# A graph attention layer: two edges to a byte before the transposes, the E row kept in PSUM, row sums divided on GpSimd and ScalarE

## The reference

```python
h = jnp.maximum(_layernorm(x, axis=-1), 0.0)
Wh = h @ W
f1 = Wh @ a[:128, 0];  f2 = Wh @ a[128:, 0]
e = jax.nn.leaky_relu(f1[:, None] + f2[None, :], negative_slope=0.2)
e = jnp.where(adj == 0, -jnp.inf, e)
out = x + jax.nn.softmax(e, axis=1) @ Wh
```

## Time and profile before

| | |
|---|---|
| median of three runs | 870.19 us |
| the profiled execution's own time | 872.21 us |
| its span | 870.5 us |
| PE busy | 841.6 us (97%) |
| PEld busy | 773.6 us (89%) |
| DVE busy | 766.2 us (88%) |
| ACT busy | 104.8 us (12%) |
| POOL busy (all of it but 0.9 us is DMA issue) | 137.0 us (16%) |
| queue of the mask loads | 67.13 MB written, 81.3% of 16 engines |
| granted TensorE clock | 0.997 of full |

### The profile page before, as it was taken

The page is one execution under the profiler, slowest core; times in us unless marked ns, Lnnn a source line. Parts: engine busy times, 40 slices in busy tenths (PEclk is TensorE's granted clock), DMA queues, the critical chain, the costliest instruction groups (busy, mean ns, idle before and its releaser), DMA issues.

```text
span 870.5 us, 23030 instructions
## 1 busy us (share of the span) xinstructions
PE 841.6 (97%) x9481; PEld 773.6 (89%) x9481; DVE 766.2 (88%) x1326; ACT 104.8 (12%) x286; POOL 137.0 (16%) x262
## 2 busy tenths in 40 slices
PE   3899999999999999999999999999999999999995
PEld 3788999999999999999999999999999999999995
DVE  4899898998989898898989889898989889898985
ACT  4788700000000000000000000000000000000000
POOL 3111111111111111111111111101110111111000
PEclk9999999999999999999999999999999999999998
DMA  9995699988998889888988998898889889988300
GB/s 219 113 107 52 59 112 87 94 92 80 95 91 90 83 91 95 81 92 87 97 83 90 91 85 92 81 103 83 90 83 94 92 81 94 93 90 82 48 2 15
DMA packets 43275, 75.95 MB, mean 87 GB/s; under 512 B 4720, under 2 KB 6896, under 8 KB 43248
## 3 DMA queue, kind: packets, MB, share of 16 engines
q0 software_dynamic: 38400, 67.13, 81.3%
q1 hardware_dynamic: 4432, 8.39, 2.9%
q10 hardware_dynamic: 416, 0.07, 0.0%
HBM read 272.70 MB, written 4.19 MB: 318 GB/s over the span
## 4 chain that ended last, share of the span: by engine, by line
PE 91%; DVE 6%; ACT 1%; DMA 1%; issue 1%; ACTq 0%; DVEq 0%
PE acc L275 50%; PE acc L279 26%; PE stage L264 13%; DVE wt_ring L620 3%; PE stage L237 1%; DVE stats L556 1%; DMA a_sb<-in_L_gnn_a_dram 1%; PE stage L224 1%; DVE pairs L611 1%; PE stage L252 1%; DVE xn L593 0%; ACT xn L399 0%; ACT wh L414 0%; DVE packed L603 0%; DVE xm L726 0%
## 5 line engine op out<-in xcount | busy, mean ns | idle before, releaser
L620 DVE SCALAR_TENSOR_TENSOR wt_ring<-row,packed,stage 128x512 f32<-128x512 uint8 (+1 forms) x1024 | 695.3, 742 | 74.9 <-PE acc L279 69.1
L275 PE MATMUL acc<-pairs,wt_ring 128*128 128x258 f16 x4096 | 720.2, 274 | 0.4 <-DVE wt_ring L620 0.2
L279 PE MATMUL acc<-pairs,wt_ring 128*128 128x129 f16 x4096 | 698.4, 219 | 0.0
L275 PEld LDWEIGHTS acc<-pairs,wt_ring 128*128 128x128 f16 x4096 | 396.2, 97 | 55.4 <-DVE wt_ring L620 0.4
L279 PEld LDWEIGHTS acc<-pairs,wt_ring 128*128 128x128 f16 x4096 | 399.5, 98 | 4.9
L178 POOL DMA_DIRECT2D masks<-in_adj_dram x252 | 133.2, 529 | 664.7 <-PE stage L264 635.7
L264 PE MATMUL stage<-ident,masks 128*128 128x128 f32 x1024 | 155.3, 275 | 2.0 <-ACT fin L483 2.0
L264 PEld LDWEIGHTS stage<-ident,masks 128*128 128x128 f32 x1024 | 108.7, 141 | 6.0 <-ACT fin L483 2.3
L513 ACT ACTIVATE fin<-acc 128x258 f32<-128x258 f32 x64 | 24.7, 386 | 730.2 <-PE acc L275 730.2
L237 PE MATMUL stage<-wx,ht 128*128 128x130 f32 x128 | 23.5, 311 | 0.7 <-ACT ht L408 0.7
L434 ACT ACTIVATE tmp<-wh,tmp 128x128 f32<-128x128 f32 x64 | 20.4, 390 | 0.4
(11 more groups left out here) (51 smaller groups left out, 80.1 us busy)
## 6 DMA issues: line engine op xcount, KB each, us to landing
masks<-in_adj_dram POOLq DMA_DIRECT2D x256, 256.0 KB, 8.8
out_dram<-xm SPq DMA_DIRECT2D x16, 256.0 KB, 2.1
xm<-in_x_dram SPq DMA_DIRECT2D x3, 1024.0 KB, 15.7
xm<-in_x_dram SPq DMA_DIRECT2D x1, 768.0 KB, 6.5
xm<-in_x_dram SPq DMA_DIRECT2D x1, 256.0 KB, 3.0
wx<-in_L_gnn_W_dram ACTq DMA_DIRECT2D x1, 64.0 KB, 3.2
a_sb<-in_L_gnn_a_dram ACTq DMA_DIRECT2D x1, 1.0 KB, 6.5
```

Of the source, the lines that this page charges most:

```text
L275: return nc.tensor.matmul(acc[:, r, 0:2 * E1], wtv[:, w, r, 1, :], pairv[:, t, :, 0:E1], start=st, stop=end)
L279: return nc.tensor.matmul(acc[:, r, 0:E1], wtv[:, w, r, 0, :], pairv[:, t, 0, 0:E1], start=False, stop=False)
L620: nc.vector.scalar_tensor_tensor(out=wt_ring[:, t % NW, :], in0=e_row, scalar=packed[:, t, 1:2], in1=marks[:, k, :], op0=ALU.max, op1=ALU. ...
```

## The change

**Edges.** The two last rows of each four-row pack (the "second" rows) are multiplied by 200, in place and as 16-bit numbers, and GpSimd adds them as 32-bit integers to the two first ones: a byte then holds a + 200 b. In group 0 and for the first four units of group 1 GpSimd does the multiplication (`second` in its block, L227), from then on ScalarE does, eight units ahead (`second`, L560). The sum is `mix` (L215). TensorE now transposes two 128x128 blocks for a unit (L368), not four. ScalarE reads the 1024 bytes of each partition from PSUM, multiplies by 1.28, adds 0.1 and writes 16-bit numbers to `marks` in SBUF (`unpack`, L549): its low byte is a, its high byte b. VectorE reads the edges from `marks`, with a step of two bytes (L774).

**E row.** `row` and its copy by ScalarE are gone. `spread` (L359) is done once in each group, after its third unit, for the next group; VectorE reads the E row straight from bank 1 or 3 of `stage`. VectorE copies the four values that it needs to `e_next` first (L791). Edges use banks 0 and 2 in the groups from 1 on and bank 0 in group 0, and transposes run two units ahead.

**Rows of output.** `finish` is gone but for the last group. GpSimd adds the halves (`sums`, L262 and L265), VectorE takes the reciprocal after the seventh unit (L848), ScalarE scales the rows after the ninth (`divided`, L583), GpSimd adds x (`outputs`, L272). **Group 0.** GpSimd takes `scaled` (L255) from ScalarE, for groups 1 to 15, and from group 4 on VectorE's half of the normalisation (L236). **Loads.** The second rows of a chunk are loaded when the chunk has been mixed, the first rows when it has been transposed.

The diff, cut to what bears on this:

```diff
--- before.py
+++ after.py
+SECOND = 200.0
+SPLIT = 256.0 / SECOND
+ABOVE = 0.1
...
-        row = sb("row", [P, N], F32)
+        marks = sb("marks", [P, MR, CHUNK], U8)
+        e_next = sb("e_next", [P, PACK], F32)
...
+            def mix(u):
+                c, k = u // KC % NC, u % KC
+                if k == 0 and u >= KC:
+                    pool.wait_ge(adj_loaded[c], (u // UN + (1 if c else 0)) * 2 * 16)
+                if u < UN + KC:
+                    pool.wait_ge(s["second_pool"], u + 1)
+                else:
+                    pool.wait_ge(s["second_ready"], u + 1 - UN - KC)
+                sl = slice(k * P, (k + 1) * P)
+                nc.gpsimd.tensor_tensor(edges4[:, c, 0, :, sl], edges4[:, c, 0, :, sl], edges4[:, c, 1, :, sl],
+                                        ALU.add).then_inc(s["mixed"], 1)
+            def second(u):
...
+                nc.gpsimd.tensor_scalar(twos[:, c, 1, :, sl], twos[:, c, 1, :, sl], SECOND, None, ALU.mult
+                                        ).then_inc(s["second_pool"], 1)
+            def sums(q):
+                pool.wait_ge(s["acc_free"], (q + 1) * PACK)
+                nc.gpsimd.tensor_scalar(fin[:, :, E1:2 * E1], fin[:, :, E1:2 * E1], 1.0 / LOW, None, ALU.mult
+                                        ).then_inc(s["lows_scaled"], 1)
+                pool.wait_ge(s["lows_scaled"], q + 1)
+                nc.gpsimd.tensor_tensor(fin[:, :, 0:E1], fin[:, :, 0:E1], fin[:, :, E1:2 * E1], ALU.add
+                                        ).then_inc(s["sums_ready"], 1)
+            for n in range(NC - 1, NQ * NC - 2):
+                if NC <= n < NQ * NC - NC:
+                    load_first(n + NC)
+                for k in range(KC):
+                    mix((n + 2) * KC + k)
+                if n + 2 + NC < NQ * NC:
+                    load_second(n + 2 + NC)
+                if n >= NC and n % NC == 0:
+                    sums(n // NC - 1)
+                if n >= NC and n % NC == 2:
+                    outputs(n // NC - 1)
...
+            def group(q, bank):
+                for b in range(UN):
+                    pe.wait_ge(s["marked"], q * UN + b + 1)
+                    transposes(b % 2 * 2, (b + 2) % UN, q * UN + b + 2)
+                    unit(q * UN + b, b, q)
+                    if b == 2:
+                        pe.wait_ge(s["weighted"], q * UN * PACK)
+                        pe.wait_ge(s["e_ready"], q + 2)
+                        spread(bank)
...
+            def unpack(bank, u, b):
+                act.wait_ge(s["transposed"], u + 1)
+                if bank or b >= MR:
+                    act.wait_ge(s["weighted"], (u + 1 - MR) * PACK)
+                nc.scalar.activation(split[:, b % MR, :].rearrange("p (s w) -> p s w", s=PACK),
+                                     stage[:, bank, 0:BANK // 2].bitcast(U8).rearrange("p (w s) -> p s w", s=PACK),
+                                     ACT.Copy, scale=SPLIT, bias=ABOVE).then_inc(s["marked"], 1)
+            def second(q, b):
...
+                nc.scalar.activation(twos[:, c, 1, :, sl], twos[:, c, 1, :, sl], ACT.Copy, scale=SECOND
+                                     ).then_inc(s["second_ready"], 1)
...
-            def weights(bank, b, e_row):
-                marks = stage[:, bank, :].bitcast(U8).rearrange("p (w s) -> p s w", s=PACK)
+            def weights(bank, b):
+                edges = marks[:, b % MR, :].rearrange("p (s w h) -> p s h w", s=PACK, h=2)
+                e_row = stage[:, bank, :].rearrange("p (h k) -> p h k", h=2)
...
-            def finish(q, step):
...
+            def rows(q, bank, more=True):
+                dve.wait_ge(s["rowp_ready"], q + 1)
+                if more:
+                    next_group(q + 1)
                 for b in range(UN):
                     u = q * UN + b
-                    dve.wait_ge(s["transposed"], u + 1)
+                    dve.wait_ge(s["marked"], u + 1)
                     dve.wait_ge(s["used"], u - 1)
-                    weights(b % 4, b, e_row)
-                    if 2 <= b <= 4:
-                        finish(q - 1, b - 2)
+                    weights(bank, b)
+                    if b == 6:
+                        dve.wait_ge(s["sums_ready"], q)
+                        nc.vector.reciprocal(inv[:], fin[:, :, Fo]).then_inc(s["inv_ready"], 1)
```

More of the change, by code:

```diff
@@ new lines, in normalise @@
+            def normalise(g):
+                pool.wait_ge(s["ln_ready"], batch_of(g) + 1)
+                pool.wait_ge(s["xt_ready"], g - 1)
+                for r in range(HALF, PACK):
+                    t = g * PACK + r
+                    ins = nc.gpsimd.tensor_scalar(xn[:, g % 2, r * P:(r + 1) * P], xm[:, g, r * P:(r + 1) * P],
+                                                  small[:, 5, t:t + 1], small[:, 6, t:t + 1], ALU.mult, ALU.add)
+                ins.then_inc(s["xn_pool"], 1)
@@ new lines, in load_second, with load_first, scaled @@
+            def load_second(n):
+                pool.wait_ge(s["mixed"], (n - NC + 1) * KC)
+                for r in (2, 3):
+                    load(n // NC, n % NC, r)
+            def load_first(n):
+                pool.wait_ge(s["transposed"], (n - NC + 1) * KC)
+                for r in (0, 1):
+                    load(n // NC, n % NC, r)
+            def scaled(g):
+                pool.wait_ge(s["exps_ready"], g + 1)
+                nc.gpsimd.tensor_tensor(tmp[:, g % 2, :, 0:Fo], wh[:, g * PACK:(g + 1) * PACK, 0:Fo],
+                                        tmp[:, g % 2, :, Fo:E1].to_broadcast([P, PACK, Fo]), ALU.mult
+                                        ).then_inc(s["scaled_ready"], 1)
@@ L189, in _, with outputs, load_rows @@
+            def outputs(q):
+                pool.wait_ge(s["fin_scaled"], q + 1)
+                y = xm[:, q, :].rearrange("p (r k) -> p r k", r=PACK)
+                nc.gpsimd.tensor_tensor(y, fin[:, :, 0:Fo], y, ALU.add).then_inc(s["rows_done"], PACK)
+            def load_rows(c):
                 pool.wait_ge(x_loaded[c + 1], 16)
@@ L191, in _ @@
                     load(0, c, r)
-            with pool.Fori(1, NQ) as q:
-                for c in range(NC):
-                    pool.wait_ge(s["transposed"], (q - 1) * UN + (c + 1) * KC)
-                    for r in range(PACK):
-                        load(q, c, r)
+            for u in range(KC):
+                second(u)
+                mix(u)
+            for c in range(1, NC):
+                load_rows(c)
+            load_second(NC)
+            for b in range(UN):
+                if b % KC == 2:
+                    load_first(NC + b // KC)
+                if b + 1 < NQ:
+                    scaled(b + 1)
+                if b + 4 < NQ:
+                    normalise(b + 4)
+                second(b + KC)
+                mix(b + KC)
+                if b % KC == KC - 1:
+                    load_second(NC + 1 + b // KC)
+            for n in range(NC - 1, NQ * NC - 2):
[9 more added lines that the diff above has]
+                    outputs(n // NC - 1)
+            outputs(NQ - 2)
             pool.wait_ge(s["flag_ready"], 1)
@@ L309, in _ @@
             features(0, 1)
-            spread(0)
-            transposes(0, 0, 0, first=True)
+            transposes(0, 0, 0)
+            pe.wait_ge(s["e_ready"], 1)
+            spread(1)
             features(1, 0)
@@ L475, in _ @@
             high_part(0)
-            keep_row(0)
+            unpack(0, 0, 0)
             keep(1, 0)
@@ L485, in _ @@
             for b in range(UN):
-                if b + 1 < NQ:
-                    scaled(b + 1)
+                if b + 1 < UN:
+                    unpack(0, b + 1, b + 1)
+                    if b + 1 >= UN + KC - AHEAD:
+                        second(1, b + 1 + AHEAD - UN)
                 if b + 3 < NQ:
@@ L504, in _ @@
                     root(3 + b // 7)
[L506 to L513 removed]
+            steady(1, 0)
+            steady(1, 1)
             act.wait_ge(s["norms_ready"], 1)
             evacuate(0)
[L517 to L519 removed]
+            with act.Fori(1, NQ - 1) as q:
+                for b in range(2, UN):
+                    steady(q, b)
+                    if b == 8:
+                        divided(q - 1)
+                steady(q + 1, 0)
+                steady(q + 1, 1)
+                evacuate(q)
+            for b in range(2, UN):
+                steady(NQ - 1, b, more=b + AHEAD < UN)
+                if b == 8:
+                    divided(NQ - 2)
+            evacuate(NQ - 1)
             act.wait_ge(s["flag_ready"], 1)
@@ L706, in _ @@
             nc.vector.tensor_scalar(lim[:, 1:2], low[:], -1.0, None, ALU.mult).then_inc(s["limits_ready"], 1)
-            dve.wait_ge(s["row_ready"], NQ)
-            with dve.Fori(1, NQ) as q:
-                rows(q)
+            with dve.Fori(0, (NQ - 2) // 2) as p:
+                rows(p * 2 + 1, 3)
+                rows(p * 2 + 2, 1)
+            rows(NQ - 1, 3, more=False)
             dve.wait_ge(s["limits_turned"], 1)
```

189 lines of the change are left out of this document (94 added, 95 removed).

## The result

The changed kernel takes 887.34 us (median of four executions, 886.64 to 889.1) against 870.34 for the kernel before: ratio 1.0201, 95% interval 1.0183 to 1.0219. The forecast was 831 us in a range from 820 to 857; the kernel is 2% slower and the time lies 30 us above the range. The profiled execution has a span of 885.1 us, against 870.5.

The account below looks back on a forecast made before the run. TensorE was taken to set the pace, with VectorE close behind. Fifteen groups save 40 us, of which 39 is kept, and group 0 counts 0: 870.2 - 39 = 831 us, range 820 to 857.

Parts of the forecast that it names:

- Two transposes less: In groups 1 to 15, two fewer edge transposes take 0.22 us a unit off TensorE: 3.125 becomes 2.905.
- what is late next: The two-unit loop between TensorE and VectorE takes 5.825 us, 2.91 a unit, about equal to TensorE's own 2.905.
- Once in each group: The E row's spread adds 0.44 us, VectorE's copy and reciprocal 0.34; a group takes 47.3 us against 50.0.
- The sum: Whole kernel: 39 us less from groups 1 to 15 and 0 from group 0, 870.2 - 39 = 831 us.
- the rival at 846 us: At group turns, queued work on ScalarE and GpSimd costs TensorE 1 us at each of 15 turns; chance 0.08.
- Clock: TensorE's clock is no question: it is granted in full in each stretch (1.00, 2.4 GHz).
- The weight instructions: VectorE's four a unit, with other operands, stay at 742 ns each, bounds 680 to 800.
- ScalarE: Unpack at 1.02 us and a multiplication at 0.63 add 1.65 of 2.91 us a unit, hidden.
- GpSimd: From group 1 on it needs 0.95 to 1.4 of 2.91 us a unit, hidden; mix about 420 ns to twice that.
- Group 0: The first group, up to about 110 us, goes from 6 us shorter to 7 longer; taken as 0.
- The rival at 840 us: GpSimd stretches group 0 by holding VectorE's two-SBUF-operand instructions: 6 us longer, 9 with the late start; chance 0.16.
- the first rival: GpSimd stretches group 0, 9 us longer with the late start, 840 us in all; chance 0.16.

Follow-up runs that it names:

- unrolled: The changed kernel with TensorE's loop of two groups written out as 14 groups in a row, no branch back; 840.49 us, 0.9651 of the kernel before.
- swap_late: swap, with ScalarE instead of GpSimd multiplying the second rows in group 0 from unit 8 on; 829.62 us, 0.9533 of the kernel before.
- swap: unrolled with chunk loads issued earlier, and GpSimd's normalisation put before the scaled features in group 0; 830.53 us, 0.9534 of the kernel before.
- before_two: The kernel before with TensorE's loop body two groups long instead of one, nothing else; 896.86 us, 1.0299 of the kernel before.
- hint: The changed kernel plus a prefetch hint for the branch that closes TensorE's loop of two groups; 852.29 us, 0.9779 of the kernel before.

## Why the prediction was wrong, point by point

From that mark, in microseconds of the profiled executions: after less before is 885.1 - 870.5 = 14.6. It is made of three parts.

| part | forecast | measured |
|---|---|---|
| groups 1 to 15, without the stalls | -40, kept 39 | -45.1 (762.3 to 717.2, in unrolled) |
| six turns of TensorE's loop | not in it | +46.9 (717.2 to 764.1) |
| group 0 | 0, from -6 to +7 | +12.8 (108.20 to 120.98) |

- **Two transposes less** and **what is late next**: right. 2.91 us a unit was forecast and is measured, and VectorE still waits a little in each.
- **Once in each group**: 47.3 us forecast, 46.94 measured in unrolled (ten groups from 262.67 to 732.09 us). The spread and copy cost 46.94 - 16 x 2.91 = 0.38, not 0.78. The right sign, half the size.
- **The sum** is the step that failed: it has no term for the six turns of TensorE's loop, which took 46.9 us. It took 15 groups at the price of a steady group, and the turns as "likely to take back as much" as the last group gives. I had looked at the turn from the side of the handshakes only (the rival at 846 us) and not at the length of TensorE's loop body, although the diff doubles it: `group(p * 2 + 1, 1)` and `group(p * 2 + 2, 3)` stand in one turn, where the kernel before has one group. A turn costs 7.7 us, since a group with one takes 54.7 us (216.07 to 270.76) and one without 47.0: 5.1 of stall and, by difference, 2.6 at half the clock. What was left for a stall that no case names was 0.03, and it decided.
- **Clock**: "no question" held only while TensorE never stopped. A stall costs more than its length. It did not hold in group 0 either, where the clock is 0.94 from 40 to 110 us (1.00 before).
- **The weight instructions**: right, 744 ns.
- **ScalarE**: right in the steady groups (1.02 and 0.62 us, 54% busy), and no turn waits for it.
- **GpSimd**: `mix` 735 ns, between the prices of 420 and twice that; the multiplication of 512 elements 1530 ns (1480 undisturbed), over its upper end of 1.4. Hidden from group 1 on, as forecast.
- **Group 0**: taken as 0, with +7 as the upper end, and it is +12.8: 6.0 from the start (`low_part` of g = 2 at 45.98, not 39.98) and 6.8 from the pace of the 13 units behind it. (The unit of 4.93 us that the sums of group 0 started from is a short one; the pace before is 5.16.) The rival at 840 us named both mechanisms. Its late start was put at 3 us, for the wait for chunk 1; the fourteen issues ahead of the first `scaled` were not counted against it, though they stand in the code in front of it. Its second mechanism is in the trace: L756 and L764 held by GpSimd. The Trainium skill's rule ("SBUF — State Buffer", section "Who interferes with whom") says so, and the trace agrees for L756 and L764, and for the weight instructions, which stay at 740 ns from 40 to 110 us. L755, with one tensor in SBUF, was held as well (1.87 us at 94 us in the changed kernel, to the end of L255). That the held instructions make up the 6.8 us is not shown (swap_late, above). I had given this rival 0.16 and counted half of a GpSimd instruction for each, which is about what the means say (0.43 us for L756).

Without the stall the forecast's terms leave little over: unrolled takes 840.49 us, the first rival's 840. That it fits so closely is luck in part: groups 1 to 15 gave 6 us more than the 39, and group 0 cost 3 to 4 more than that rival's 9. The 830.53 of swap is near the forecast by two edits of group 0 that the change doesn't contain, and with the loop written out.

What stays open: from which length of the loop body the stall begins; why it is 5 us or more in the changed kernel and 3 in before_two, whose body is no shorter (its 26 us over the kernel before are 4.3 for each of six turns); why the clock falls behind some stalls and not behind others of nearly the same length; and what sets the pace of group 0.

## What to carry to other kernels

Count the instructions of each engine's loop body before and after a change, as one counts an engine's time: a body that has doubled can cost at its turns what the change saves inside, and written-out code gets it back (47 us here), a hint most of it (35 us). When an idle engine is given arithmetic beside VectorE, check which VectorE instructions run at the same moment and whether the same semaphore releases both. When an issuing queue gets arithmetic, look for what stands in front of the first result that others wait for.

## What the runs showed of the hardware

- A jump back of TensorE over a body of two groups: 5.0 to 6.4 us without a hint, 1.4 to 1.9 with one (3.0 to 3.5 in before_two). After each of the six long stalls pairs of matmuls run at 1.2 GHz for 2.6 to 5.3 us, after four of before_two's six for 3.6 us, after hint's only behind the one of 1.94 us.
- GpSimd's multiplication of 512 uint16 values by a constant takes 1.48 us, ScalarE's 0.62.
- VectorE's instructions of 8 elements were stretched from 0.17 to as much as 1.9 us. Most of those that took 0.9 us or more ended within 0.2 us of the end of GpSimd's two-operand L255, also where they had begun beside the load issue ahead of it. Beside load issues that L255 did not follow they kept their 0.17 (65.96 us in swap); beside the one-operand multiplication L227 some kept it (111.65 us in the changed kernel) and others took 0.53 to 0.57.
